# Expert layers of a fused attention and mixture-of-experts kernel: the weights of five of the eight experts are loaded after the routing instead of beside it

## The reference

```
x = x + ffn(layernorm(x))
# ffn, for T = 2048 tokens, E = 8 experts, F = 512, capacity C = 256:
probs = softmax(xt @ router_w);  gate = max(probs);  idx = argmax(probs)
pos   = cumsum(onehot(idx)) - 1          # place of the token within its expert
h     = relu(expert_inputs @ w1 + b1)    # per expert: 256x128 @ 128x512
y     = h @ w2 + b2                      # per expert: 256x512 @ 512x128
out   = y of the token's expert * gate   # tokens past the capacity get 0
```

## Time and profile before

| | us |
|---|---|
| median of 3 runs | 1132.87 |
| lowest, highest | 1132.27, 1138.27 |
| the profiled execution itself | 1134.53 |
| its span | 1132.8 |
| PE busy | 976.8 (86%) |
| DVE busy | 766.6 (68%) |
| ACT busy | 595.5 (53%) |
| POOL busy | 331.5 (29%) |

### The profile page before, as it was taken

One profiled execution on the slowest core, in us unless ns is written; L12 is line 12 of the kernel. 1 busy time (PEld: TensorE's weight loads), 2 busy tenths in 40 slices (PEclk: granted clock), 3 DMA queues, 4 the chain that ended last, 5 costly groups with the idle time before them and its releaser, 6 DMA issues. The chain is left out here.

```text
span 1132.8 us, 18698 instructions
## 1 busy us (share of the span) xinstructions
PE 976.8 (86%) x6218; PEld 628.0 (55%) x6218; DVE 766.6 (68%) x2268; ACT 595.5 (53%) x1176; POOL 331.5 (29%) x420
## 2 busy tenths in 40 slices
PE   6999999999999999999638567889999999997382
PEld 4766677676767666666437424344444444434372
DVE  6776757775777757675612699787988888854422
ACT  4766667675766657664212363415555555564120
POOL 3522122112222112210235006543454434311522
PEclk9999999999999999999659589868999999998586
DMA  6630000000000000000621100000000000001523
GB/s 209 133 86 2 1 2 1 1 1 1 2 1 1 1 1 2 1 1 1 180 64 38 38 0 1 1 1 1 1 2 1 1 2 1 1 1 43 164 58 94
DMA packets 49356, 32.25 MB, mean 28 GB/s; under 512 B 9147, under 2 KB 45932, under 8 KB 49260
## 3 DMA queue, kind: packets, MB, share of 16 engines
q1 hardware_dynamic: 47212, 26.78, 8.4%
q0 software_dynamic: 2048, 4.26, 1.1%
HBM read 21.44 MB, written 11.69 MB: 29 GB/s over the span
## 5 line engine op out<-in xcount | busy, mean ns | idle before, releaser
L618 ACT ACTIVATE attn_a_prob<-attn_a_score,attn_a_m_all 128x128 f32<-128x128 f32 (+7 forms) x256 | 188.8, 740 | 52.5 <-DVE attn_a_m_all L541 48.9
L968 ACT ACTIVATE attn_b_probT<-attn_b_st 128x1024 f32<-128x1024 f32 (+1 forms) x192 | 145.1, 808 | 131.7 <-PE attn_b_st L834 130.4
L537 DVE TENSOR_REDUCE attn_a_m_far<-attn_a_score 128x1 f32<-128x512 f32 (+3 forms) x192 | 105.7, 550 | 65.0 <-PE attn_a_score L449 62.8
L461 PE MATMUL attn_a_slot<-tab,attn_a_prob 128*128 128x128 f32 x1152 | 149.6, 274 | 0.0
L473 PE MATMUL attn_a_o<-attn_a_ptsb,Vd 128*64 128x512 f32 x288 | 140.6, 606 | 0.0
L473 PE MATMUL attn_a_o<-attn_a_ptsa,Vd 128*64 128x512 f32 x288 | 140.5, 606 | 0.0
L461 PEld LDWEIGHTS attn_a_slot<-tab,attn_a_prob 128*128 128x128 f32 x1152 | 132.0, 141 | 10.6 <-issue 3.2
L897 DVE CUSTOM_DVE_ANT_0 attn_b_slot<-attn_b_slot,later 128x128 f32<-128x128 f32 (+3 forms) x256 | 118.6, 522 | 18.7 <-PE attn_b_slot L809 18.5
L809 PE MATMUL attn_b_slot<-KS,attn_b_alone 128*128 128x512 f32 (+2 forms) x384 | 124.8, 421 | 3.6 <-POOL attn_b_alone L990 2.4
L627 ACT ACTIVATE attn_a_ptsa<-attn_a_slot 128x512 f32<-128x512 f32 x144 | 85.7, 595 | 65.2 <-PE attn_a_slot L461 64.8
L541 DVE CUSTOM_DVE_ANT_0 attn_a_score<-attn_a_score,bias_near,attn_a_m_far 128x256 f32<-128x256 f32 (+2 forms) x192 | 107.4, 559 | 7.0 <-DVE attn_a_m_far L537 0.2
(11 more groups left out here) (233 smaller groups left out, 1851.3 us busy)
## 6 DMA issues: line engine op xcount, KB each, us to landing
moe_weights_w<-in_L_ffn_w_dram SPq DMA_DIRECT2D x32, 256.0 KB, 4.2
to_experts<-xn SPq DMA_DIRECT2D x2, 1056.0 KB, 11.7
moe_experts_xe<-to_experts SPq DMA_DIRECT2D x16, 132.0 KB, 2.4
bias_by_query_and_key<-bias_by_distance SPq DMA_DIRECT2D x2, 1024.0 KB
bias_near<-bias_by_query_and_key SPq DMA_DIRECT2D x2, 1024.0 KB, 6.1
from_experts<-xn SPq DMA_DIRECT2D x2, 1024.0 KB, 11.6
moe_experts_back<-from_experts SPq DMA_DIRECT2D x8, 256.0 KB, 3.8
X<-in_L_attn_a_x_dram SPq DMA_DIRECT2D x2, 512.0 KB, 4.6
```

The source lines that it names most:

```text
L461: ins = nc.tensor.transpose(dst[:, jj * P:(jj + 1) * P], probs(g)[:, 2 * jj + half, i * P:(i + 1) * P], ident[:, :])
L537: nc.vector.tensor_reduce(least, score[t % 2][:, at:at + nk - win], AX.X, ALU.min).then_inc(far_done, 1)
L618: nc.scalar.activation(probs(g)[:, j, 0:nk], score[t % 2][:, at:at + nk], ACT.Exp, bias=m_all[:, j:j + 1], scale=-1.0, accum_out=rowsum[g ...
L968: nc.scalar.activation(probT[n % 2][:, two, lo:], st[:, two, lo:], ACT.Exp, scale=-1.0).then_inc(exp_done, 1)
```

## The change

`loads` is given the semaphore `placed` of the routing. SP issues the nine DMAs of experts 0 to 2 at the head as before. Ahead of the first DMA of expert 3 it waits until `placed` is 4, which the `place` of the last chunk brings. Then it issues the fifteen DMAs of experts 3 to 7. Nothing else is changed, and both expert layers are built by this code.

```diff
@@ dispatch
-        loads(block)
+        loads(block, placed)
@@ build
+        FIRST = 3
+
         def moe(name, k):
...
-                def loads(block):
+                def loads(block, placed):
 
                     @block.sync
                     def _(sp):
                         for e in range(E):
+                            if e == FIRST:
+                                sp.wait_ge(placed, TILES // BLK)
                             sp.dma_start(w1[:, e, :], t["w1"][e]).then_inc(weights[e], 16)
```

## The result

| | before | after |
|---|---|---|
| median, 18 runs each, us | 1135.29 | 1143.70 |
| lowest, highest | 1130.64, 1138.37 | 1138.94, 1145.24 |
| profiled execution, us | 1134.53 | 1143.71 |
| its span | 1132.8 | 1141.8 |
| mean granted clock | 0.918 | 0.916 |

The ratio is 1.0072, with a 95% interval of 1.0055 to 1.0088, so the change costs some 8.2 us; the medians lie 8.4 us apart. The forecast was +4.6 us and 1137.5 us (range to 1141.0).

The account below looks back on a forecast made before the run. The path was taken to run from last place through last scatter and barrier to token load, with PE waiting. Per layer +1.9 landing and +0.4 tail, twice +2.3 = +4.6 on 1132.9 gave 1137.5 us; range 1130.5 to 1141.0.

Parts of the forecast that it names:

- Steps 1 and 2: SP, first layer: released at 572.97, issues the held weights in 8.1 us, done at 581.1; cost 0.
- Step 3: Weight transfer: five experts, 2.95 MB, are through 11.7 us after the first issue.
- Step 5: SP's queue, first layer: stream ends at 585.9; token loads, issued at 582.83 into the same queue, stand behind it.
- steps 6 and 7: First token load: lands at 586.9, +1.9 us; engines finishing unevenly add 0 to +0.7, taken as +0.4, per layer.
- the last scatter is held back: POOL's 16th scatter lands 2.6 us later under the stream, delaying the token load; +5.4 to +6.8 us, 1139.0 us; chance 0.22.
- Nothing gained at the head of the routing: Up to 567 us, 15 weight DMAs leave; early scatters land sooner but nobody waits for them; valued at 0.
- The stall: DVE's unexplained 4.63 us wait at chunk 2's place, both layers; taken as staying, rival says it goes: 1129.5 us, chance 0.17.
- Clock: PE's first expert matmuls: a later start shifts the clock level, -1.6 to +1.6 us a layer; taken as 0.

Follow-up runs that it names:

- loaded_twice: Kernel before, with experts 3 to 7 loaded a second time once the last chunk has its places; PE waits for both: 1139.88 us, ratio 1.0076.
- behind_tokens: Changed kernel, but SP issues experts 3 to 7 in the second phase, behind the eight token loads: 1130.63 us, ratio 1.0005.
- act_queue: Changed kernel, but ACT issues the fifteen held weight DMAs on its own queue: 1137.55 us, ratio 1.0061.
- hold_all: Changed kernel, but all eight experts are held until the last chunk has its places: 1144.12 us, ratio 1.012.
- placed_one: Changed kernel, but the five experts are held only until the first chunk has its places: 1130.89 us, ratio 1.0011.
- before_again: Kernel before, unchanged, run once more for a profile beside the second set: 1129.78 us (one run).
- hold_two: Changed kernel, but only experts 6 and 7 are held: 1130.70 us, ratio 1.0006.
- hold_three: Changed kernel, but only experts 5 to 7 are held: 1132.42 us, ratio 1.0016.

## Why the prediction was wrong

**Steps 1 and 2 (release and issue, cost 0): right.** The last place ended at 575.31, SP began at 575.34 and was done at 584.21, 8.9 us instead of 8.1. POOL ends later.

**Step 3 (the stream's length): right.** 575.34 to 588.2 by its packets, 12.9 us, and 13.6 in the second layer; forecast 12.9 with the scatters (11.7 + 1.2).

**Step 5 (the token load is issued at 582.83 and stands behind the stream): this failed.** It took POOL's last issue for the end of the scatter and left the barrier where it was. The barrier waits until the scatter has landed: POOL's closing instruction of the phase ends 3.0 to 3.1 us after the last issue in kernels without the stream there and 6.5 to 7.1 with five experts' stream, each time 0.76 us after that scatter's last recorded landing. The token load follows 0.9 us later (1.2 once). So it came 3.8 and 3.5 us later, when the stream was all but over, and steps 6 and 7 (landing +1.9, tail +0.4) found nothing left to act on: 2.25 us to the landing. Twice 2.3 was forecast and 7.3 came; loaded_twice, behind_tokens and act_queue show it. The 1.0 us that step 6 sets between the stream's end and the landing (0.4 of transfer and 0.6 for which it names no row) did come in hold_all, where the load queues: 1.0 in both layers. Only the time of the issue was wrong. That the kernel came out slower, as forecast, speaks for another mechanism than step 5's.

**The rival "the last scatter is held back": right in mechanism, small in price.** Its sign was named (token load issued at 585 or later, landing in 2.3) and came. It stood at 2.7 to 3.4 us a layer and 1139.0 us in all; 3.5 to 3.8 and 1143.7 were measured. Its lower end rested on the first packet; the barrier waits for the last. It got 0.22 on the ground that the stream is only 6 us old at the last scatter, "with less issued and not moved". The forecast's own rows refute that. SP issues 2.95 MB in 8.1 us, 2.2 MB in 6. The engines move 0.09 MB in the first 2 us and 0.97 in the next 4. That leaves 1.1 MB, and after 10 us 3.64 - 2.32 = 1.3 MB. A backlog is nearly full within 6 us. The trace of the change has it at 1.12 MB 3.8 us after SP's first held DMA and at 1.31 MB after 5.1.

The rule of the Trainium skill, "DMA: Bandwidth & Descriptors", on queues, rings and completion order, by which an engine takes turns between queues packet by packet, would have made this rival free. The runs disagree for SP's queue as for ACT's: with 1.2 to 1.3 MB of weights ahead of the scatter in q1 or q10 the seam is 7.4 to 8.0 us. Where the scatter waits meanwhile no trace shows.

**Nothing gained at the head of the routing: right.** behind_tokens frees the same stretch and placed_one its first 10 us, and they stand at 1.0005 and 1.0011.

**The stall is not the weights' (kept at 0): right, for a reason that the forecast couldn't know.** It stands in the first pair's profiles, in before and after alike, and in none of the eleven that came later from two chips, those with every weight at the head included (which chip the first pair ran on is not on record). The 16 KB fetch of the earlier trace rows isn't enough for it either: in before_again one passes too, at 563 to 564 us, and DVE waits 0.54 us. What the wait is stays open. The medians of before, 1135.3 us beside the first pair and 1130.1 to 1130.8 in the later sets, would fit with it, which is argued and not shown.

**The median.** Three runs gave 1132.87 for before, 18 gave 1135.29. So 2.4 us of the miss of 6.2 lie in the starting point and 3.8 in the mechanism.

**Clock (0, range +-1.6 a layer): held.** +0.4 and 0.0 us for the first matmuls in the first pair, +0.9 and +1.4 in the second.

**Two slips in the sums, without effect.** The second layer's landing, 1082.0 against 1080.19, is +1.8 and not +1.9. Half of 0.22 and a sixth of 0.44 are 0.18, not the 0.21 given for more than 5.7 us slower.

No version beat the kernel before; hold_two, placed_one and behind_tokens equal it within the noise.

## What to carry to other kernels

In this kernel a bulk transfer issued ahead of a small one that the path needs delayed it by about the bytes that were issued and not yet moved, over the rate, and it made no difference whether the bulk was in SP's queue or in ACT's. Work out that backlog at the small transfer's issue, not only the stream's end, and add some tenths for a stream that is just ending (hold_three). Put the bulk so early that it is over by then, or behind the last transfer on which something waits. And where a phase ends on an engine whose last act is a DMA, look in the trace whether its end is the issue or the landing: here it was the landing.

## What the runs showed of the hardware

Scatters of q0 were served about in the order of issue beside q1 and q10: no packet for 2.7 to 4.8 us behind 1.0 to 1.49 MB, against 1.5 us with none. POOL's closing of a phase came from 3.0 to 7.1 us after its last issue, always 0.76 us after the landing where no other engine was later. A token load queued behind the weights in its own queue landed 1.0 us after their last packet (hold_all). An unnamed wait of DVE of 4.6 us, in place or in pieces of 2.5 to 4.0, was in both profiles of the first pair and in none of eleven later ones.
